# Deformable convolution on one core: the sampling matrices are split pixel by pixel and turned by DMA, and the pipeline works in steps twice as large

## The chip, the cores and the metric

One core of a Trainium2 chip. The metric is the device time of one execution in microseconds (us): 4269.75 us for the kernel before, the median of 3 runs (4259.26 to 4272.78).

## What is computed

The input is a batch of 32 images of 192 channels and 32 x 32 pixels in f32. Cut to what matters:

```python
x = x + attention(groupnorm(x))            # 4 heads' channel attention: q, k, v, softmax over channels, out
v = groupnorm(x)
offset = clip(conv3x3(v, off_w) + off_b, -8, 8)          # 2 x 9 values per pixel
mask = 2 * sigmoid(conv3x3(v, mask_w) + mask_b)          # 9 values per pixel
y = deformable_conv3x3(v, offset, mask, proj_w) + proj_b # bilinear samples at the shifted taps, times weights
x = x + gelu(batchnorm(y))                 # batchnorm: mean and variance over all 32 images
```

## The kernel before

The images go one after another through a loop of two images per turn (`images`, L336 to L349). The deformable convolution is written as matrix products. For an image's chunk of 128 pixels (4 rows, 8 chunks) and each row of taps ky, **Z** = the pixels times the projection weights of three taps (576 columns) is made by TensorE (`z_product`, L628 to L640), in two halves of 288 columns. **S** is the sampling matrix: for each output pixel and tap, the bilinear weight on each of 256 pixels around it (8 rows). It is an outer product of a row part `ay` and a column part `bx`, and GpSimd makes it with the output pixel on the partitions (`sT`, L1323). TensorE needs the source pixel on the partitions, so it turns S with f32 transposes against an identity matrix (`turn_s`, L642 to L651, three of 128 x 128 per unit) into a PSUM bank. Both S and Z are then kept as two f16 halves: ScalarE casts to the high half (`split_s` L883, `split_z` L848), VectorE subtracts it from the f32 value for the low half (`split_s` L1139, `split_z` L1134). `s_product` (L662 to L670) adds nine products of 192 columns into one accumulator bank.

The unit of work is one (tile of output pixels, ky, chunk c): 48 units for an image. In unit u TensorE turns S of unit u + 2, waits for both halves of S of unit u, multiplies, and makes Z of group u + 10 (`part1`, L728 to L754). The other engines keep the same order in queues of their own. Two PSUM banks hold Z and two hold turned S, so TensorE can be two groups ahead of the halves' makers. Every six units a tile of 128 output pixels is done: ScalarE copies the accumulator out (L906 to L910) and the next tile's first product waits for that (`y_pm`, L658).

**Preparation of the next image** (`part0`, one function on each engine) is cut into the same 48 units and interleaved: in unit u of image b every engine does part u of image b + 1. The parts with work: 0 to 5 statistics; 6 to 10 normalisation and its halves (ScalarE four passes of 1024 columns); 12 to 22 attention up to the combined matrix, a chain that goes to and fro between TensorE, ScalarE and VectorE; 23 to 29 the result x1 and its statistics; 30 to 36 the second normalisation, its halves and shifted copies (VectorE, `move`); 38 and 39 the offset convolution (216 products on TensorE); 40 to 46 the row and column parts of S ("hats": `ay`, `bx`). Three more column hats of the current image are made at units 4, 16 and 28 (`column_hats`). SyncE loads x of the next image and stores x1 and y. After all images the batchnorm constants are made, and a last stage streams y and x1 through the core.

Each image ends with a branch on a flag: only if an offset is larger than the 256 pixels allow is `far_pass` run. With these inputs no instruction of it is in the trace.

Of the kernel before, what the change touches and what calls it, by code (L numbers as in the profile page):

```python
# [35 lines left out]
P = 128  # L36
C, H, W = 192, 32, 32
N = H * W
CB = C - P
# [12 lines left out]
UNITS = 6 * TILES  # L52
HEAD_SCALE = float((C // 4) ** (-0.5))
# [29 lines left out]
def build(nc, x, w_qkT, w_v, w_outT, b_out, w_off, b_off, w_proj, proj_b, gamma, beta,  # L83
# [6 lines left out]
    with ExitStack() as ctx:  # L90
# [94 lines left out]
        zps = bank("zps", (P, 2, 512))  # L185
        sps = [bank(f"sps{i}") for i in range(2)]
# [56 lines left out]
        s_ps = sem("s_ps")  # L243
        s_hi = sem("s_hi")
        s_lo = sem("s_lo")
        sz_done = sem("sz_done")
# [89 lines left out]
        def images(program, eng):  # L336

            part0, part1, weights_ready = program  # L340
            for u in range(SLOTS):
                part0(u, 0, 0)
                if u == 15:
                    weights_ready()
            part1(0, 0, True)
            with eng.Fori(1, NB - 2, 2) as b:
                part1(b, 1, True)
                part1(b + 1, 0, True)
            part1(NB - 1, (NB - 1) % 2, False)  # L349
# [7 lines left out]
        AHEAD = 10  # L357
        FAR_Z = 2 * AHEAD
        FAR_SLOT = S_RING - 1
# [8 lines left out]
        def z_piece(z, g, par):  # L368

            half = g % 2 * (KO // 2)  # L370
            return z[:, tile_at(g // 6, par), g % 6 // 2, half:half + KO // 2]
# [37 lines left out]
        def _(sp):  # L409
# [12 lines left out]
            def attended(b, more=True):  # L422
                sp.wait_ge(x1_sb, 4 * b + 4)
                sp.dma_start(x1_dram[b, 0:P], x1[:, 0]).then_inc(x1_stored, 16)
                sp.dma_start(x1_dram[b, P:C], x1[0:CB, 1]).then_inc(x1_stored, 16)
                if more:
                    load_x(b + 1)

            def convolved(b):
                sp.wait_ge(y_final, b + 1)  # L430
                sp.dma_start(y_dram[b, 0:P], ych[:, 0]).then_inc(y_stored, 16)
                sp.dma_start(y_dram[b, P:C], ych[0:CB, 1]).then_inc(y_stored, 16)

            attended(0)
            with sp.Fori(1, NB - 2, 2) as b:
                attended(b)
                convolved(b - 1)
                attended(b + 1)
                convolved(b)
            attended(NB - 1, False)  # L440
            convolved(NB - 2)
# [21 lines left out]
            convolved(NB - 1)  # L463
# [19 lines left out]
        def _(pe):  # L483
# [136 lines left out]
            def z_group(g, b, par):  # L620
# [3 lines left out]
                if g >= 2 or not first(b):  # L624
                    pe.wait_ge(z_lo, UNITS * b + g - 1)
                z_product(g, par, par).then_inc(z_ps, 1)

            def z_product(g, par, of):  # L628

                j, ky = tile_at(g // 6, par), g % 6 // 2  # L630
# [3 lines left out]
                o = zps[:, g % 2, 0:KO // 2]  # L634
                n = slice(g % 2 * KO // 2, (g % 2 + 1) * KO // 2)
                pe.matmul(o, at(0), wpr_h[:, 0, ky, n], start=True, stop=False)  # L636
                pe.matmul(o, at(0), wpr_l[:, 0, ky, n], start=False, stop=False)  # L637
                pe.matmul(o, at(1), wpr_h[:, 0, ky, n], start=False, stop=False)  # L638
                pe.matmul(o, at(2), wpr_h[:, 1, ky, n], start=False, stop=False)  # L639
                return pe.matmul(o, at(2), wpr_l[:, 1, ky, n], start=False, stop=True)  # L640

            def turn_s(u, b):  # L642
                t, ky, c = u // 6, u % 6 // 2, u % 2
                if c == 0:
                    pe.wait_ge(st_made, 24 * b + 3 * t + ky + 1)
                if u >= 2 or not first(b):
                    pe.wait_ge(s_lo, UNITS * b + u - 1)
                g = (3 * t + ky) % ST_RING
# [4 lines left out]
            def convolve(u, b, par):  # L653
                i, ky, c = u // 6, u % 6 // 2, u % 2
                pe.wait_ge(s_lo, UNITS * b + u + 1)
                if i + c < CHUNKS and (c == 1 or i == 0):
                    pe.wait_ge(z_lo, UNITS * b + 6 * (i + c) + 2 * ky + 2)
                if u % 6 == 0 and (i > 0 or not first(b)):  # L658
                    pe.wait_ge(y_pm, TILES * b + i)
                s_product(u % S_RING, tile_at(i + c, par), ky, u % 6 == 0, u % 6 == 5).then_inc(sz_done, 1)  # L660

            def s_product(slot, j, ky, start, stop):  # L662

                for kx in range(3):
                    z = slice(kx * C, (kx + 1) * C)
                    s_h, s_l = sh[:, slot, kx], sl[:, slot, kx]
# [17 lines left out]
            def far_pass(b, par, more):  # L684
                pe.wait_ge(s_lo, UNITS * (b + 1) + 2 * more)
# [10 lines left out]
                if more:  # L696
                    pe.wait_ge(z_lo, UNITS * (b + 1) + AHEAD)
                    first_chunks(par, 0)
                    pe.wait_ge(fz_lo, FAR_Z * b + AHEAD)
                for t in range(TILES):  # L700
                    for ky in range(3):
                        pe.wait_ge(f_st, 24 * b + 3 * t + ky + 1)
                        for v in far_of(t, ky):
# [3 lines left out]
                            for kx in range(3):  # L707
                                mm = pe.transpose(sps[v % 2][:, kx * P:(kx + 1) * P],
# [681 lines left out]
```

## Time and profile before

| | us |
|---|---|
| median of the runs | 4269.75 |
| span of the profiled execution | 4284.4 |
| TensorE busy, share | 3630.2, 85% |
| VectorE | 2649.3, 62% |
| ScalarE | 2110.5, 49% |
| GpSimd | 1410.9, 33% |
| mean granted TensorE clock | 0.939 of full speed |

The profiled execution's own time is its span, 4284.4 us; it lies 14.65 us above the median of the runs. PE is TensorE, ACT ScalarE, DVE VectorE, POOL GpSimd, SP SyncE; L650 is line 650 of the kernel before.
### The profile page before, as it was taken

The page shows a single profiled execution, that of the slowest core. Times are in us where ns is not written, and L with a number is a line of the kernel's source. Part 1 is how long each engine was busy: PE and PEld are TensorE (multiplying, and loading weights), DVE is VectorE, ACT ScalarE, POOL GpSimd, SP SyncE. Part 2 cuts the span into 40 slices and gives each one's busy share as a digit, 9 for nine tenths or more (in the row PEclk, how much of TensorE's full clock was granted, in tenths as well). Part 3 has the DMA queues.
Part 4 walks back from the last instruction along what each step waited for, and adds up shares of the span by engine and source line. Part 5 has one row for each costly group of instructions (what it writes and reads, how often), then busy time and mean ns, then how long its engine had stood idle before and what let it go on. Part 6 is the DMA issues. An engine that isn't in the chain of part 4 may idle for free.

```text
span 4284.4 us, 109949 instructions
## 1 busy us (share of the span) xinstructions
PE 3630.2 (85%) x38338; PEld 3094.4 (72%) x38338; DVE 2649.3 (62%) x5834; ACT 2110.5 (49%) x4790; POOL 1410.9 (33%) x1165
## 2 busy tenths in 40 slices
PE   3999898999989899998989989898998989899700
PEld 2787777877777778777777877777787777778700
DVE  3666666666666666666666666666666666666522
ACT  1555554555455455545545554554555455445432
POOL 1333332333333233333333333333333333333311
PEclk8999999999999999999999999999999999999955
DMA  2000000000000000000000000000000000000298
GB/s 59 18 27 10 28 27 20 27 27 27 10 27 27 20 27 26 27 10 27 27 20 27 26 27 16 21 27 20 27 26 27 21 16 27 27 20 16 60 361 301
DMA packets 50975, 172.85 MB, mean 40 GB/s; under 512 B 9664, under 2 KB 10880, under 8 KB 50176
## 3 DMA queue, kind: packets, MB, share of 16 engines
q1 hardware_dynamic: 39584, 136.75, 10.6%
q0 software_dynamic: 7168, 25.17, 1.5%
q8 instruction: 426, 6.98, 0.7%
q14 instruction: 373, 3.06, 0.2%
q10 hardware_dynamic: 3424, 0.90, 0.1%
HBM read 87.29 MB, written 75.50 MB: 38 GB/s over the span
## 4 chain that ended last, share of the span: by engine, by line
PE 63%; DVE 13%; issue 13%; ACT 4%; DMA 4%; DVEq 1%; ACTq 1%; SPq 1%; POOL 0%; POOLq 0%
PE sps L650 10%; PE acc L667 6%; PE acc L668 6%; PE acc L669 6%; PE l L578 4%; PE zps L636 3%; DVE zl L1136 3%; PE zps L640 3%; PE zps L637 3%; PE zps L638 3%; PE zps L639 3%; DMA xn<-x_scratch 2%; DVE sl L1142 2%; DVE ych L1204 2%; PE l L510 1%
## 5 line engine op out<-in xcount | busy, mean ns | idle before, releaser
L1323 POOL TENSOR_TENSOR sT<-ay,bx 128x768 f32<-128x768 f32 x768 | 1148.1, 1505 | 1615.3 <-PE sps L650 1547.9
L1142 DVE TENSOR_TENSOR sl<-sps,sh 128x384 f16<-128x384 f32 x1536 | 847.1, 552 | 743.7 <-ACT sh L887 740.3
L887 ACT CAST sh<-sps 128x384 f16<-128x384 f32 x1536 | 741.7, 483 | 915.4 <-PE sps L650 905.9
L667 PE MATMUL acc<-zh,sh 128*128 128x192 f16 x4608 | 1155.7, 251 | 0.3 <-ACT ypm L910 0.3
L668 PE MATMUL acc<-zl,sh 128*128 128x192 f16 x4608 | 1155.5, 251 | 0.0
L669 PE MATMUL acc<-zh,sl 128*128 128x192 f16 x4608 | 1155.2, 251 | 0.0
L650 PE MATMUL sps<-eye,sT 128*128 128x128 f32 x4608 | 808.0, 285 | 322.0 <-issue 218.2
L853 ACT CAST zh<-zps 128x288 f16<-128x288 f32 x1536 | 620.1, 404 | 699.6 <-PE zps L640 672.6
L1136 DVE TENSOR_TENSOR zl<-zps,zh 128x288 f16<-128x288 f32 x1536 | 693.9, 452 | 423.0 <-ACT zh L853 415.7
L650 PEld LDWEIGHTS sps<-eye,sT 128*128 128x128 f32 x4608 | 544.5, 143 | 451.9 <-issue 229.4
L667 PEld LDWEIGHTS acc<-zh,sh 128*128 128x128 f16 x4608 | 459.0, 100 | 37.5 <-issue 35.9
L668 PEld LDWEIGHTS acc<-zl,sh 128*128 128x128 f16 x4608 | 459.1, 100 | 20.9
L669 PEld LDWEIGHTS acc<-zh,sl 128*128 128x128 f16 x4608 | 459.1, 100 | 1.6
L636 PE MATMUL zps<-wpr_h,x_hi_a 128*128 128x288 f16 x1344 | 392.1, 292 | 0.8 <-DVE zl L1136 0.3
L637 PE MATMUL zps<-wpr_l,x_hi_a 128*128 128x288 f16 x1344 | 390.8, 291 | 0.0
L638 PE MATMUL zps<-wpr_h,x_lo_a 128*128 128x288 f16 x1344 | 390.1, 290 | 0.0
L639 PE MATMUL zps<-wpr_h,x_hilo_b 128*128 128x288 f16 x1344 | 389.7, 290 | 0.0
L640 PE MATMUL zps<-wpr_l,x_hilo_b 128*128 128x288 f16 x1344 | 389.7, 290 | 0.0
L1307 POOL TENSOR_TENSOR bx<-off,cx_sb 128x576 f32<-128x576 f32 x128 | 155.3, 1213 | 459.4 <-DVE off L1103 459.4
L1289 POOL TENSOR_TENSOR rstd<-gvar,mhalf 128x2 f32<-128x2 f32 x64 | 44.8, 700 | 582.0 <-DVE gvar L993 582.0
L578 PE MATMUL l<-wof,x2s_hi_a 128*128 128x54 f16 x1536 | 183.0, 186 | 9.8 <-DVE x2w_hilo_b L1009 9.8
L578 PE MATMUL l<-wof,x2s_lo_a 128*128 128x54 f16 x1536 | 182.8, 186 | 0.0
(200 smaller groups left out, 6498.0 us busy)
## 6 DMA issues: line engine op xcount, KB each, us to landing
xin<-in_x SPq DMA_DIRECT2D x32, 512.0 KB, 5.5
xin<-in_x SPq DMA_DIRECT2D x64, 256.0 KB, 5.9
x_scratch<-x SPq DMA_DIRECT2D x32, 512.0 KB, 2.8
y_scratch<-ych SPq DMA_DIRECT2D x32, 512.0 KB, 2.7
zh<-y_scratch SPq DMA_DIRECT2D x20, 512.0 KB, 11.0
zl<-x_scratch SPq DMA_DIRECT2D x20, 512.0 KB, 12.0
out<-zh POOLq DMA_DIRECT2D x20, 512.0 KB, 8.8
x_scratch<-x SPq DMA_DIRECT2D x32, 256.0 KB, 3.5
```

The source lines that it names most:

```text
L578: mm = pe.matmul(o, src[:, row * W:(row + ROWS_T) * W], wof[:, m, k].rearrange("p i j -> p (i j)"), start=(k == 0 and n == 0), stop=(k == ...
L636: pe.matmul(o, at(0), wpr_h[:, 0, ky, n], start=True, stop=False)
L637: pe.matmul(o, at(0), wpr_l[:, 0, ky, n], start=False, stop=False)
L650: mm = pe.transpose(sps[u % 2][:, kx * P:(kx + 1) * P], sT[:, g, kx, c * P:(c + 1) * P], eye32[:, :])
L667: pe.matmul(acc[:, 0:C], s_h, zh[:, j, ky, z], start=start and kx == 0, stop=False)
L668: pe.matmul(acc[:, 0:C], s_h, zl[:, j, ky, z], start=False, stop=False)
L669: mm = pe.matmul(acc[:, 0:C], s_l, zh[:, j, ky, z], start=False, stop=stop and kx == 2)
L853: act.copy(z_piece(zh, g, par), zps[:, g % 2, 0:KO // 2]).then_inc(z_hi, 1)
L887: act.copy(sh[:, u % S_RING].rearrange("p k n -> p (k n)"), sps[u % 2][:, 0:3 * P]).then_inc(s_hi, 1)
L1136: dve.tensor_tensor(z_piece(zl, g, par), zps[:, g % 2, 0:KO // 2], z_piece(zh, g, par), ALU.subtract)\
L1142: dve.tensor_tensor(one(sl), sps[u % 2][:, 0:3 * P], one(sh), ALU.subtract).then_inc(s_lo, 1)
L1323: pool.tensor_tensor(sT[:, p % ST_RING].rearrange("p k (r x) -> p k r x", r=R), a, x_, ALU.mult)\
```

## The change

The transposes on TensorE go away. GpSimd now makes S with all 256 source pixels of three taps in one f32 tile (as before), ScalarE and VectorE split it into f16 halves where it lies, 768 columns at once, and SyncE turns both halves, 1536 columns of f16, with one DMA transpose into `sT`. Work goes in 24 steps of what were two units. Z is made as 2 x 288 columns in two neighbouring PSUM banks and its halves are made 576 columns at once. Look-ahead is 5 steps for Z and 3 for S (4 for GpSimd). The ring of f32 S and the ring of its halves have 2 places each, the ring of turned S has 4. Preparation is shifted by 6: step p of image b does parts 2p + 6 and 2p + 7 of image b + 1, and from step 21 on the first six parts of image b + 2; both parts stand together behind the step's products. SyncE issues nothing but transposes during the images; loads of x and stores of x1 and y move to ScalarE's queue (x1 and x at part 34, y at step 5). The column hats of the current image are made at steps 1, 7 and 13. GpSimd's reserved scratch for descriptors is 4096 bytes instead of the default.

```diff
+STEPS = 3 * TILES
+SHIFT = 6
...
-        ST_RING = 3
-        sT = sb("sT", [P, ST_RING, 3, R * W])
-        S_RING = 3
-        sh = sb("sh", [P, S_RING, 3, P], F16)
-        sl = sb("sl", [P, S_RING, 3, P], F16)
+        S_RING = 2
+        s32 = sb("s32", [P, S_RING, 3 * R * W])
+        spm = sb("spm", [P, S_RING, 2, 3 * R * W], F16)
+        T_RING = 4
+        sT = sb("sT", [P, T_RING, 12, P], F16)
...
-        zps = bank("zps", (P, 2, 512))
-        sps = [bank(f"sps{i}") for i in range(2)]
+        zps = bank("zps", (P, 4, 512))
...
+        def prepare(part0, u, b, par, more):
+
+            if u + SHIFT < SLOTS:
+                if more:
+                    part0(u + SHIFT, b + 1, 1 - par)
+            elif more == 2:
+                part0(u + SHIFT - SLOTS, b + 2, par)
...
-        AHEAD = 10
+        AHEAD = 5
+        S_AHEAD = 3
...
+            def turn_s(p, b):
+                sp.wait_ge(s_lo, STEPS * b + p + 1)
+                sp.sem_inc(lo_seen, 1)
+                if p >= T_RING or not first(b):
+                    sp.wait_ge(sz_done, STEPS * b + p - T_RING + 1)
+                    sp.sem_inc(slot_free, 1)
+                sp.dma_start_transpose(sT[:, p % T_RING], spm[:, p % S_RING].rearrange("p i n -> p (i n)"))\
+                  .then_inc(turned(b, p)[0], 16)
...
-            def turn_s(u, b):
...
-                for kx in range(3):
-                    mm = pe.transpose(sps[u % 2][:, kx * P:(kx + 1) * P], sT[:, g, kx, c * P:(c + 1) * P], eye32[:, :])
-                mm.then_inc(s_ps, 1)
...
+            def convolve(p, b, par):
+                i, ky = p // 3, p % 3
+                pe.wait_ge(*turned(b, p))
+                if p % 3 == 0 and (i > 0 or not first(b)):
                     pe.wait_ge(y_pm, TILES * b + i)
...
+                for p in range(STEPS):
+                    convolve(p, b, par)
+                    if p == 4:
+                        offset_max(b)
+                    if p + AHEAD < STEPS:
+                        z_group(p + AHEAD, b, par)
                     elif more:
...
+                        z_group(p + AHEAD - STEPS, b + 1, 1 - par)
+                    if p % 6 == 1 and p > 6:
+                        turn_y(p // 6 - 1, b)
+                    for u in (2 * p, 2 * p + 1):
+                        prepare(part0, u, b, par, more)
...
+                if u == 34:
+                    store_x1(b)
+                    if not isinstance(b, int) or b < NB - 1:
+                        load_x(b + 1)
...
+            def split_s(p, b):
+                act.wait_ge(st_made, STEPS * b + p + 1)
+                if p >= S_RING or not first(b):
+                    act.wait_ge(*turned(b, p - S_RING))
+                act.copy(spm[:, p % S_RING, 0], s32[:, p % S_RING]).then_inc(s_hi, 1)
...
+                        split_s(p + S_AHEAD - STEPS, b + 1)
...
+                    if p % 6 == 1 and p < 18:
+                        column_hats(p // 6 + 1, b, par)
+                    if p % 3 == 2:
+                        t = p // 3
+                        act.wait_ge(sz_done, STEPS * b + p + 1)
...
+            def split_s(p, b):
+                dve.wait_ge(s_hi, STEPS * b + p + 1)
+                dve.tensor_tensor(spm[:, p % S_RING, 1], s32[:, p % S_RING], spm[:, p % S_RING, 0], ALU.subtract)\
+                   .then_inc(s_lo, 1)
...
+                if p >= S_RING or not first(b):
+                    pool.wait_ge(s_lo, STEPS * b + p - S_RING + 1)
...
-    nc = bacc.Bacc("TRN2", target_bir_lowering=False, num_devices=1)
+    nc = bacc.Bacc("TRN2", target_bir_lowering=False, num_devices=1, dynamic_dma_scratch_size=4096)
```

## Rows read from the trace of the kernel before

**Rows 1.** One image: stretch, length, busy PE, PEld, DVE, ACT, POOL, clock, DMA share, GB/s.

```profile
1059.50:1182.70 123.20, 112.99 (x1198) 96.18 (x1198) 80.54 (x181) 64.26 (x150) 42.61 (x34) 0.97 0.08 24
```

**Rows 2.** Timeline of TensorE through one unit (start, duration).

```profile
1062.54 0.49 PE L650 MATMUL sps<-eye,sT 128*128 128x128 f32 x3
...
1062.87 0.25 PE L667 MATMUL acc<-zh,sh 128*128 128x192 f16 x1
...
1063.61 0.29 PE L636 MATMUL zps<-wpr_h,x_hi_a 128*128 128x288 f16 x1
...
1064.22 0.49 PE L650 MATMUL sps<-eye,sT 128*128 128x128 f32 x3
```

**Rows 3.** Waits of TensorE in one image (1236.0 to 1357.5): total, times, longest.

```profile
PE sps L650 <- issue: 8.4, 1, 8.4
...
PE l L509 <- DVE gram L1056: 0.6, 1, 0.6
```

**Rows 4.** Stretches of parts 30 to 37 and 40 to 47 of one image.

```profile
1311.65:1328.51 16.86, 14.29 (x138) 12.27 (x137) 14.45 (x27) 11.58 (x24) 9.53 (x8) 1.00 0.12 24
1338.10:1352.80 14.70, 13.98 (x141) 12.27 (x137) 10.16 (x30) 9.92 (x26) 8.74 (x7) 1.00 0.01 2
```

**Rows 5.** ScalarE's timeline: hats, an eviction, casts and normalisation.

```profile
1246.73 0.69 ACT L844 ACTIVATE bx<-bx 128x576 f32<-128x576 f32 x1
...
1250.15 0.32 ACT L909 COPY ypm<-acc 128x192 f32<-128x192 f32 x1 [0.26 <-PE acc L669]
...
1250.69 0.40 ACT L853 CAST zh<-zps 128x288 f16<-128x288 f32 x1
...
1253.81 0.47 ACT L887 CAST sh<-sps 128x384 f16<-128x384 f32 x1
1254.17 0.41 ACT L853 CAST zh<-zps 128x288 f16<-128x288 f32 x1
1254.46 1.26 ACT L777 ACTIVATE xh_a<-xin,nbias,rstd 128x1024 f16<-128x1024 f32 x1
1255.60 0.48 ACT L887 CAST sh<-sps 128x384 f16<-128x384 f32 x1
```

**Rows 6.** Groups of the whole run: busy, mean ns of one, idle before.

```profile
L1142 DVE TENSOR_TENSOR sl<-sps,sh 128x384 f16<-128x384 f32 x1536 | 847.1, 552 | 743.7 <-ACT sh L887 740.3
L887 ACT CAST sh<-sps 128x384 f16<-128x384 f32 x1536 | 741.7, 483 | 915.4 <-PE sps L650 905.9
...
L853 ACT CAST zh<-zps 128x288 f16<-128x288 f32 x1536 | 620.1, 404 | 699.6 <-PE zps L640 672.6
L1136 DVE TENSOR_TENSOR zl<-zps,zh 128x288 f16<-128x288 f32 x1536 | 693.9, 452 | 423.0 <-ACT zh L853 415.7
```

**Rows 7.** Timeline of the softmax, parts 18 to 21: VectorE and ScalarE.

```profile
1282.00 0.61 DVE L1042 TENSOR_REDUCE nmax<-l 128x1 f32<-128x192 f32 x2 [0.89 <-PE l L510]
...
1284.12 0.43 ACT L812 ACTIVATE gram<-l,nmaxs 128x192 f32<-128x192 f32 x1
...
1286.65 1.05 DVE L1056 TENSOR_SCALAR gram<-gram,rinv 128x192 f32<-128x192 f32 x2
```

**Rows 8.** DMAs: issue of three loads on SyncE; issue to landing, median us.

```profile
1181.45 2.15 SPq L412 DMA_DIRECT2D xin<-in_x  x3
...
xin<-in_x SPq DMA_DIRECT2D x64, 256.0 KB, 5.9
x_scratch<-x SPq DMA_DIRECT2D x32, 512.0 KB, 2.8
```

**Rows 9.** A 2-us window of TensorE, idle since 1227.7: granted clock 0.94.

```profile
1230.00:1232.00 2.00, 0.00 (x0) 0.94 0.07 12
```

**Rows 10.** The same copy on VectorE beside GpSimd and without it.

```profile
1071.87 1.69 POOL L1323 TENSOR_TENSOR sT<-ay,bx 128x768 f32<-128x768 f32 x1 [2.23 <-PE sps L650]
...
1072.16 1.45 DVE L1008 COPY x2w_hi_a<-x_hi_a 128x96 f16<-128x96 f16 x1
...
1080.32 0.17 DVE L1008 COPY x2w_hilo_b<-x_hilo_b 128x96 f16<-128x96 f16 x1
```

More of the change, by code:

```diff
@@ L242, in build @@
         st_made = sem("st_made")
-        s_ps = sem("s_ps")
         s_hi = sem("s_hi")
         s_lo = sem("s_lo")
+        lo_seen = sem("lo_seen")
+        slot_free = sem("slot_free")
+        s_turned = [sem(f"s_turned{i}") for i in range(T_RING)]
         sz_done = sem("sz_done")
@@ L420, in _, with part1 @@
             sp.dma_start(cx_sb[:, :, :], cx.rearrange("p (k x) -> p k x", k=TAPS)).then_inc(const_in, 16)
[L422 to L441, printed above, removed]
+            def turn_s(p, b):
[6 more added lines that the diff above has]
+                  .then_inc(turned(b, p)[0], 16)
+            def part1(b, par, more):
+                if first(b):
+                    for p in range(S_AHEAD):
+                        turn_s(p, b)
+                for p in range(STEPS):
+                    if p + S_AHEAD < STEPS:
+                        turn_s(p + S_AHEAD, b)
+                    elif more:
+                        turn_s(p + S_AHEAD - STEPS, b + 1)
+            images((lambda u, b, par: None, part1, lambda: None), sp)
             def load(dst, src, q, slot, i):
@@ L848, in split_z @@
             def split_z(g, b, par):
[L849 to L853 removed]
+                if g % 3 == 0 and not first(b):
+                    act.wait_ge(sz_done, STEPS * (b - 1) + 3 * (last_use(g // 3) + 1))
+                act.wait_ge(z_ps, STEPS * b + g + 1)
+                act.copy(z_piece(zh, g, par), z_bank(g)).then_inc(z_hi, 1)
             def far_pass(b, par, more):
[L856 removed]
+                act.wait_ge(sz_done, STEPS * (b + 1))
                 act.wait_ge(yt_ps, 4 * (b + 1))
@@ L910, in part1 @@
                         act.copy(ypm[:, t % 4, C:2 * P], acc[:, P:C]).then_inc(y_pm, 1)
-                    if u + AHEAD < UNITS:
-                        split_z(u + AHEAD, b, par)
+                    if p + AHEAD < STEPS:
+                        split_z(p + AHEAD, b, par)
                     elif more:
-                        split_z(u + AHEAD - UNITS, b + 1, 1 - par)
-                    if more:
-                        part0(u, b + 1, 1 - par)
+                        split_z(p + AHEAD - STEPS, b + 1, 1 - par)
+                    for u in (2 * p, 2 * p + 1):
+                        prepare(part0, u, b, par, more)
+                    if p == 5 and not first(b):
+                        store_y(b - 1)
                 where_far(flag, act, b, par, more, far_pass, (fz_hi, FAR_Z), (fs_hi, FAR_UNITS), (fy_pm, TILES))
@@ new lines, in part1 @@
+            def part1(b, par, more):
+                lead = S_AHEAD + 1
+                if first(b):
+                    for p in range(lead):
+                        make_s(p, b, par)
+                for p in range(STEPS):
+                    if p + lead < STEPS:
+                        make_s(p + lead, b, par)
+                    elif more:
+                        make_s(p + lead - STEPS, b + 1, 1 - par)
+                    if p in (0, 4, 10):
+                        column_distance((0, 4, 10).index(p) + 1, b, par)
+                    for u in (2 * p, 2 * p + 1):
+                        prepare(part0, u, b, par, more)
```

227 lines of the change are left out of this document (99 added, 128 removed).

## Prediction

> **What bounds the kernel now.** I read the busy time of an image first. TensorE works 113.0 of 123.2 us, VectorE 80.5, ScalarE 64.3, GpSimd 42.6 [rows 1]. So TensorE sets the pace, and I looked at what it does in a unit and at what it waits for. The timeline of a unit shows 0.33 us of transposes (start to start), 0.74 of products with S, 0.61 of Z: 1.68 in all, 80.6 us for the 48 units of an image [rows 2]. TensorE's waits in an image are one fetch of instructions of 8.4 us at the loop's turn (about half that at the other image end), 0.6 us for the softmax [rows 3], 2.6 us in the second normalisation (16.86 less 14.29) and 0.7 us with the hats [rows 4]. In those last two stretches VectorE and ScalarE are nearly full: 14.5 and 11.6 of 16.9 us. That is the row to remember: TensorE is the bound on average, but not everywhere by much.
>
> **What TensorE saves.** 144 transposes of an image go: 48 x 0.33 = 16 us. A step costs 2 x (0.74 + 0.61) = 2.7 us where two units cost 3.36. If nothing else moved, 31 images would give 500 us.
>
> **What the other engines pay.** In a full queue ScalarE starts a cast of S every 0.36 us, one of Z every 0.29, a normalisation pass every 1.14 [rows 5]. The slope from 288 to 384 columns is 0.82 ns a column on ScalarE and 1.04 on VectorE [rows 6]. So a 768-wide cast costs 0.36 + 384 x 0.82 ns = 0.68, a 576-wide one 0.53; on VectorE (0.47 and 0.36 now, durations less the same 0.09 of overlap) 0.87 and 0.66. That is a little less than today in all: 29 us for 31 on ScalarE, 37 for 40 on VectorE. Totals stay far under 107 us; they decide nothing. The order in the queues does, because a step now carries two preparation parts at once and has 20% less TensorE time over it. I walked the queues of one image with these costs, three times where it matters.
>
> *Step 3.* The first product of a tile waits until ScalarE has copied out the tile before. ScalarE's queue from the image's start: Z's cast can begin at 2.85 us (the first step's end); cast 0.53; parts 6 and 7, two passes 2.3; cast of S 0.7; hats 2 x 0.68 = 1.36 [rows 5]; cast of Z 0.53; parts 8 and 9, 2.3; cast of S 0.7; eviction 0.54 [rows 5]: 11.8 us. TensorE arrives after 3 x 2.68 = 8.0. It waits 3.8 us. Today the hats stand at unit 4, before an eviction that has no passes ahead of it, and nothing is waited for.
>
> *Steps 5 to 8, attention.* Parts of a pair now follow each other with no product between. Part 20 (VectorE) and 21 (TensorE) share step 7: behind part 18's product come the maxima (0.61 and a small scaling, with the product's own tail 1.0), the exponentials (two of 0.43 and their sums, 0.92) [rows 7], ScalarE's cast of S, hats and cast of Z (0.7 + 1.35 + 0.53), VectorE's half of Z 0.66 and the scaling (1.05 and the reciprocals, 1.3) [rows 7]: 6.5 us and some 0.4 of semaphores. TensorE has 1.5 + 1.2 + 0.45 us to do, so it waits 3.7, where it waits 0.6 now. Parts 22 and 23 share step 8: a cast and a subtraction with a small one behind each, 1.7 us, hidden by a whole unit today. Parts 16 and 17: 1.2 us for 0.5.
>
> *Steps 12 to 16.* The four passes meet the hats of step 13 again. From the end of step 12: cast of Z 0.53, two passes 2.3, cast of S 0.7, hats 1.35, cast of Z 0.53, two passes 2.3, cast of S 0.7, eviction 0.54, together 9.0; TensorE is at the next tile after two steps, 5.4, and waits 3.4 to 3.6. In step 14 ScalarE also issues five DMAs, 3.2 us in its queue (three take 2.15 on SyncE [rows 8]), with its casts and thereby VectorE's copies behind them; the offset convolution then waits for the last copy, 2.8 us. Together 6.2 for 2.6 now [rows 4].
>
> *Steps 17 to 21.* Parts 40 and 41, 44 and 45 share steps, so ScalarE stands waiting for VectorE's offsets and distances (some 2 us twice by the walk) with its casts queued behind it, and the hats of part 42 besides; a late half of Z (0.7), a late turn (0.9) and a late eviction (3.3) cost 4.9 us for 0.7 now. *Group statistics* at steps 11 and 23: 3.0 for about 0.8.
>
> Waits in all 3.8 + 3.7 + 1.7 + 1.2 + 6.2 + 4.9 + 3.0 = 24.5 us where today's walk gives 5: 19.5 more, against 16 less: **+3.3 us an image**. The same walk over today's order gives waits of about 1.1, 0.3 and 1.1 us at units 36 to 38, which is how the 2.6 us of [rows 4] come about.
>
> *The clock.* TensorE had been idle for about 4 us (since 1227.7) when the granted clock began to fall from 2.4 GHz, 0.94 in that window [rows 9]. The new waits end just short of that; I add 0.2 us an image.
>
> **Costed at nothing.** The fetches at the image ends stay: branch and loop are the same. SyncE has only 24 transposes an image in 127 us. GpSimd's tile (1.5 us a step) is released by VectorE and stays ahead. The later load of x (part 34 instead of 28) still leaves seven steps. The stores of y at step 5 are 1 us of ScalarE's queue behind an eviction. The smaller scratch and the untouched last stage give nothing. If a cover fails, it is ScalarE's: each us there before an eviction is a us of TensorE.
>
> *The turn itself* has no row. It moves 384 KB: the nearest rows are a store of 512 KB, 2.8 us to landing, and a load of 256 KB behind another, 5.9 [rows 8]. I take 3.5, nearer to the store, since nothing is queued ahead of it. A place in the ring of halves is used every second step: 5.4 us in the shortest steps less 1.6 of casts, more in the long ones, so up to about 5 us it costs nothing; at 5.9 about 1.5 us an image; below 2.8 it gains nothing. The Trainium skill (DMA: Bandwidth & Descriptors, "Latency and other measured facts") states 261 GB/s for one kernel's DMA transposes; as an estimate from that page 384 KB would move in 1.5 us, and the sum would be the same. No run here shows it.
>
> **VectorE and GpSimd.** A copy of 96 columns took 1.45 us instead of 0.17 and ended with GpSimd's multiplication, at 1073.56 [rows 10]: one of the two stood still until the other was done. The new subtraction of S has both inputs in SBUF, while today's has one in PSUM. So it costs 0.87 alone and up to 1.48 more if GpSimd's tile has just begun. I take 0.87, because GpSimd starts its tile when a subtraction ends, three engines' turns before the next. The Trainium skill (SBUF — State Buffer, "SBUF: two separate sides") says that a VectorE operation with two SBUF inputs and a GpSimd operation hold a shared port in turn, for a whole instruction; by that rule every subtraction is exposed, and the trace agrees for the copy.
>
> **The sum.** 31 images x 3.5 = +109. The first starts 4 us later (a transpose must land). The last has no preparation beside it, so it saves most of the 16: -12. +101 on the profiled 4284, which is 15 above the median: 4370.
>
> **Rivals.**
> *TensorE keeps the pace (faster).* The place is the three evictions (3.8 + 3.4 + about 3.3 us). If ScalarE reaches them in time, 10.5 us fall away and an image takes 7 less: 4370 - 31 x 10.5 = 4045. For it: ScalarE is busy only half the time. Against: 11.8 us of queue over 8.0. It decides from 3.3 us an image on. 22%.
> *VectorE meets GpSimd.* If a subtraction waits on average 0.55 us, 13 us of VectorE an image, half of it in stretches that are late, +6: 4560. 10%.
> *The turn is the bound.* Where a transpose holds the queue for more than a step, 24 of them are the image: at 6.5 us, 156 us an image and 5300; it decides from 5.3 us a transpose on. The Trainium skill (VectorE: DVE Perf Modes, "The three transpose paths") gives 1309 ns for 128 x 128 by DMA and 390 on TensorE; twelve in a row would be 15.7 us, an estimate from the page that speaks against the change. Nothing in the rows bears out that they go one by one. 6%.
> *No difference:* the transposes leave TensorE but new waits give back just the 16 us, 4270: the change does not do what it says. 6%.
>
> **How the numbers follow.** Forecast 56%, rivals 22, 10, 6, 6. A measurement of this kernel tells 0.3%, 13 us. Faster 22%, within 6%, slower 72%. Its own range is 4300 to 4460 (a us of error an image and the landing's bounds). To leave out no more than two in ten it reaches down to 4120, which leaves out about half of the faster rival, and up to 4600, over VectorE's.
>
> **What would show it.** Right: an image of 126 to 128 us; TensorE busy near 97 of it; waits of products (first of a tile) for ScalarE's copy of the accumulator, 3 to 4 us, three an image; one of 3 to 4 for the scaled softmax; offset convolution waiting for VectorE's copy; transposes landing in 3 to 5 us. Wrong: images under 120 us with those waits absent, products waiting for the DMA instead, or subtractions of S at 1.3 us and more.

## The result and the profile after

The changed kernel takes **4540.5 us** (median of 4 runs, 4512.4 to 4557.7) beside 4268.8 for the kernel before (4259.3 to 4272.8): ratio 1.064, 95% interval 1.060 to 1.068. Slower, as forecast (4370, range 4120 to 4600), but by 272 us where the sum had 101.

The page of the changed kernel: the span, the busy times, TensorE's granted clock and the DMA engines in slices, and DMA queue 1, which carries the transposes.

```profile
span 4556.1 us, 93343 instructions
PE 3341.9 (73%) x33730; PEld 2754.6 (60%) x33730; DVE 2420.0 (53%) x4298; ACT 1903.8 (42%) x3254; POOL 1421.9 (31%) x1165
PEclk8888889898888989888898988889888988998955
DMA  2545556454655555465555555555545555555699
q1 hardware_dynamic: 1220272, 356.77, 47.1%
```

TensorE is at work for less time than before, the DMA engines are half busy all the way, and the clock row shows more 8s than 9s. How much that is, a stretch of 24 images tells, cut at the same point of the softmax in both kernels. First the kernel before, then the changed one (columns as in [rows 1]):

```profile
410.81:3400.68 2989.87, 2714.73 (x28755) 2315.96 (x28754) 1933.10 (x4320) 1535.38 (x3553) 1022.84 (x816) 0.97 0.08 24
```

```profile
430.99:3635.95 3204.96, 2499.21 (x25299) 2063.86 (x25297) 1758.46 (x3168) 1378.96 (x2401) 1029.88 (x816) 0.89 0.55 92
```

Divided by 24, an image took 124.6 us, TensorE busy 113.1 and idle 11.5; it takes 133.5 now, busy 104.1 and idle 29.4. So 9.0 us more an image; 31 images make 278, nearly all of the 272. The sum had busy 16 us less and idle 19.5 us more.
TensorE's waits over the whole run (total, times, longest) answer to [rows 3]:

```profile
PE acc L687 <- ACT ypm L941: 332.6, 96, 4.3
PE acc L687 <- issue: 190.4, 31, 9.8
PE l L535 <- DVE gram L1089: 90.2, 32, 3.4
PE l L604 <- issue: 74.5, 21, 5.8
PE l L590 <- DVE mt_l L1095: 48.9, 32, 1.5
PE l L604 <- DVE x2w_hilo_b L1042: 27.3, 32, 9.8
```

Three waits an image for the copied accumulator (L941), 10.4 us together (forecast 3.8 + 3.4 + 3.3); the softmax 2.8 (3.7); parts 22 and 23 1.5 (1.7). The stalls at the image ends, which the prediction took for fetches of instructions, are still there (second row). New and not in the sum is the fourth row: in the middle of the offset convolution (L604) TensorE stands still for about 3.5 us in two images of three, and this view names nothing that it waited for.

What a wait does to the clock: windows of 1 us around the wait for the accumulator at step 15, 1415.0 to 1418.1 (second number: busy TensorE; third last: granted clock).

```profile
1414.00:1415.00 1.00, 1.00 (x9) 0.59 (x6) 0.26 (x1) 1.00 (x3) 0.65 (x1) 1.00 0.02 8
1415.00:1416.00 1.00, 0.03 (x1) 0.00 (x0) 1.00 (x2) 1.00 (x2) 0.83 (x1) 1.00 0.79 135
...
1417.00:1418.00 1.00, 0.00 (x0) 0.00 (x0) 1.00 (x5) 1.00 (x4) 0.00 (x0) 0.94 1.10 280
1418.00:1419.00 1.00, 0.92 (x6) 0.88 (x7) 1.00 (x2) 0.57 (x2) 0.23 (x1) 0.50 1.03 401
```

Nearly 3 us after TensorE went idle the clock drops to 1.2 GHz, and the next 3.4 us of products run at it. At the softmax (TensorE idle from 1378.3) it drops after 2.0 us already:

```profile
1378.30:1380.30 2.00, 0.04 (x1) 0.00 (x0) 1.10 (x3) 1.21 (x2) 1.12 (x1) 1.00 0.11 22
1380.30:1381.10 0.80, 0.00 (x0) 0.00 (x0) 0.69 (x5) 0.00 (x0) 0.36 (x1) 0.52 1.13 210
1381.10:1387.10 6.00, 5.97 (x24) 3.82 (x25) 0.96 (x1) 1.26 (x3) 0.00 (x1) 0.50 0.19 34
```

The length of a wait alone does not settle it. The softmax wait is 2.8 us in 31 of the 32 images. The clock falls 2.0 to 2.5 us into it in some, 0.4 to 2.3 us after TensorE is at work again in others, and in three not at all. Over the 24 images 112 waits of 2.6 to 4.5 us began at full clock: 53 had the fall inside, 50 up to 2.5 us behind them, 9 had none. Of 104 waits of 0.35 to 1.3 us none had a fall at either place.

Finally the landings: the extremes over 558 transposes (min, median, max).

```profile
DMA to landing us min/median/max: 3.6/3.7/14.4
```

The median is close to the 3.5 that was taken. But two transposes an image, issued 3.6 and 8.1 us after the first of the five transfers of part 34 (two stores of x1, three loads of x), land after 10 to 14 us; the last of the three loads takes 12.7 in the median.

### The profile page after: what moved, and what is told of

It is laid out like the page before. It is cut to its first block, busy times and chain, and to the rows that moved or that the text cites. A ratio compares the mean times of both kernels' runs of the same rounds, so it can differ in the third digit from the quotient of the medians.

```text
span 4556.1 us, 93343 instructions
## 1 busy us (share of the span) xinstructions
PE 3341.9 (73%) x33730; PEld 2754.6 (60%) x33730; DVE 2420.0 (53%) x4298; ACT 1903.8 (42%) x3254; POOL 1421.9 (31%) x1165
## 4 chain that ended last, share of the span: by engine, by line
PE 41%; issue 17%; DVE 15%; ACT 11%; DMA 7%; DVEq 4%; ACTq 4%; SPq 1%; POOL 0%; POOLq 0%
PE acc L687 5%; PE acc L688 5%; PE acc L689 5%; PE l L604 3%; DMA sT<-spm 3%; ACT zh L870 3%; ACT spm L903 3%; DVE stats L1007 2%; PE zps L663 2%; PE zps L664 2%; DMA xn<-x_scratch 2%; PE zps L665 2%; PE zps L667 2%; PE zps L666 2%; ACTq L862 2%
## 5 line engine op out<-in xcount | busy, mean ns | idle before, releaser
L1354 POOL TENSOR_TENSOR s<-ay,bx 128x768 f32<-128x768 f32 x768 | 1136.2, 1481 | 2392.3 <-DVE spm L1174 2006.4
L687 PE MATMUL acc<-zh,sT 128*128 128x192 f16 x4608 | 1237.3, 269 | 558.7 <-ACT ypm L941 332.6
L1174 DVE TENSOR_TENSOR spm<-s,spm 128x768 f16<-128x768 f32 x768 | 757.3, 986 | 1107.9 <-ACT spm L903 903.0
L688 PE MATMUL acc<-zl,sT 128*128 128x192 f16 x4608 | 1239.5, 269 | 20.5 <-issue 20.5
L689 PE MATMUL acc<-zh,sT 128*128 128x192 f16 x4608 | 1239.4, 269 | 0.0
L870 ACT CAST zh<-zps 128x576 f16<-128x576 f32 x768 | 489.6, 638 | 1039.1 <-PE zps L667 1038.5
L1169 DVE TENSOR_TENSOR zl<-zps,zh 128x576 f16<-128x576 f32 x768 | 579.5, 754 | 592.7 <-ACT zh L870 588.9
L687 PEld LDWEIGHTS acc<-zh,sT 128*128 128x128 f16 x4608 | 491.1, 107 | 661.4 <-ACT ypm L941 322.0
L903 ACT CAST spm<-s 128x768 f16<-128x768 f32 x768 | 638.5, 832 | 589.7 <-DMA sT<-spm 396.4
L688 PEld LDWEIGHTS acc<-zl,sT 128*128 128x128 f16 x4608 | 492.8, 107 | 49.8 <-issue 23.1
L689 PEld LDWEIGHTS acc<-zh,sT 128*128 128x128 f16 x4608 | 496.7, 108 | 8.4
L604 PE MATMUL l<-wof,x2s_hi_a 128*128 128x54 f16 x1536 | 187.6, 189 | 27.3 <-DVE x2w_hilo_b L1042 27.3
L604 PE MATMUL l<-wof,x2s_hilo_b 128*128 128x54 f16 x1536 | 187.1, 188 | 3.1 <-issue 3.1
L604 PE MATMUL l<-wof,x2s_lo_a 128*128 128x54 f16 x1536 | 187.2, 189 | 2.1 <-issue 2.1
L604 PE MATMUL l<-wof,x_hi_a 128*128 128x54 f16 x768 | 145.0, 189 | 50.4 <-issue 50.4
L604 PEld LDWEIGHTS l<-wof,x2s_hi_a 128*128 128x128 f16 x1536 | 137.0, 98 | 56.3 <-DVE x2w_hilo_b L1042 36.8
```

Source lines behind the costliest of these rows:

```text
L604: mm = pe.matmul(o, src[:, row * W:(row + ROWS_T) * W], wof[:, m, k].rearrange("p i j -> p (i j)"), start=(k == 0 and n == 0), stop=(k == ...
L687: pe.matmul(acc[:, 0:C], s_h, zh[:, j, ky, z], start=start and kx == 0, stop=False)
L688: pe.matmul(acc[:, 0:C], s_h, zl[:, j, ky, z], start=False, stop=False)
L689: mm = pe.matmul(acc[:, 0:C], s_l, zh[:, j, ky, z], start=False, stop=stop and kx == 2)
L870: act.copy(z_piece(zh, g, par), z_bank(g)).then_inc(z_hi, 1)
L903: act.copy(spm[:, p % S_RING, 0], s32[:, p % S_RING]).then_inc(s_hi, 1)
```

## The experiments

Each kernel was timed in three rounds beside the kernel before; its time is read against that kernel's 4273 to 4277 us in the same rounds, and against the change's ratio of 1.064. The change's own runs lie 45 us apart, so differences between two variants are good to some 20 us.

### Is it the clock?

Useless products ahead of four waits, into a bank that is free there:

```diff
+FILLS = 4
...
+def keep_busy(bank, n):
+    for _ in range(n):
+        pe.matmul(bank[:, 0:2 * C], eye32[:, :], wqk[:, 0], start=True, stop=True)
...
 # convolve
+if p in (3, 15, 21):
+    ...
+    keep_busy(l0[1 if p == 3 else 0], FILLS)
...
 # part 21
+keep_busy(l0[1], FILLS - 1)
 pe.wait_ge(prob_sb, b + 1)
```

> The changed kernel, and TensorE does useless f32 products (four of 384 columns, 2.6 us; three ahead of the softmax) just before the four places where it waits 2.8 to 4.1 us for another engine; nothing else differs. Clock theory: the missing time is the granted clock, which falls to 0.5 5.5 times an image (once in the kernel before) and stretches TensorE's busy time from the 97 us that the sum had to 104. The dips behind these four waits go, those behind the two fetch stalls stay: 3 dips an image or fewer, mean clock 0.92 or more, useful TensorE work about 4 to 5 us an image shorter, 4400 to 4460 us. If part of what is gained turns into longer waits at ScalarE's queue, 4480. Rival (the waits and the transposes' traffic themselves are the price, the clock is only their sign): 4540, or slower by what the products overrun, up to 4580.

Measured: **4416.0 us** (4397.6 to 4450.2), 1.031 (1.027 to 1.036): more work on the engine that bounds the kernel, and 125 us less. 24 images of it:

```profile
416.66:3536.07 3119.41, 2600.47 (x26019) 2098.05 (x26017) 1772.86 (x3168) 1376.73 (x2400) 1031.64 (x816) 0.93 0.57 95
```

Busy 108.4 us an image, of which the 15 products are 9.7 (0.65 each from one start to the next), leaves 98.6 for the useful work against 104.1: 5.5 us. The clock falls 2.1 times an image for 5.5, and is at half for some 17 us for 29. The useful products are the same, and their time fell together with the half-clock time; the theory stands. Of the 5.5 us, 1.9 came back as longer waits, most of them in the offset convolution: 2.3 us an image for VectorE's copies (0.9 before), and 110.7 us in all in the unnamed stall (74.5 before). So filling does not touch that stall.

### Is it the order of the queues?

The shift of preparation is one constant (`SHIFT = 7`, `SHIFT = 3`).

> The changed kernel with image preparation shifted by 7 units instead of 6, so that parts are paired 21+22, 41+42, 43+44 and not 20+21, 22+23, 40+41, 44+45. Queue theory (where ScalarE's passes and hats fall against the evictions sets the waits): the walk of the queues gives 4.4 us an image less wait, with fewer dips of the clock on top 6 to 8: 4300 to 4400 us. Rival (the waits come from the transposes themselves, their landing or their traffic, or from the wider steps whatever the pairing): within 1% of the changed kernel, 4500 to 4580.

> The changed kernel with image preparation shifted by 3 units instead of 6. Queue theory: the walk gives 5.4 us an image less wait than with 6; with fewer dips of the clock 4280 to 4400 us, about as the shift by 7. Rival (a larger shift is what hides the softmax and the moved copies): slower than the changed kernel, 4560 to 4650, since the copies of x2 reach the first step of the next image 1.5 steps later. Rival (transposes and not the order): 4500 to 4580.

Measured: **4459.7** (1.042, 1.038 to 1.047) for 7, above the 4300 to 4400 expected; **4404.0** (1.029, 1.025 to 1.033) for 3, at the edge. Both are better than 6. The walk's 4.4 and 5.4 us an image less wait came out as 3.2 and 5.4 us of image time, but that is not the walk's doing alone: in neither trace does TensorE stall in the offset convolution without a named cause, which is 2.4 us an image of the 4.3 and 4.1 us of idle time that went. (The expectation for the run with 36 dummy transposes, below, says that both showed that stall; their waits do not have it.) So the order of the queues gave clearly less than the walk had, and why the stall is absent no run shows. The clock stayed at 0.89 and 0.90, with 5.5 and 4.6 falls an image. Fewer waits are no gain in clock as long as those left are long: with 7, the wait for the accumulator at step 15 alone grew from 3.0 to 6.3 us.

The shift alone, in the kernel before:

> The kernel before with one part of the change alone: image preparation runs 6 units earlier, S is still turned by TensorE, units stay single. The walk of the queues gives an image 1 us longer than before: 4270 to 4330 us. If instead the shift by itself is what brings ScalarE's passes onto the evictions, 3 to 5 us an image: 4370 to 4430. If the shift is a gain that the rest of the change gives back: 4200 to 4250.

Measured: **4290.2** (1.0044, 1.0030 to 1.0058; 10 runs). Clear of noise, but 0.4% only, as the walk had it: moving the preparation costs next to nothing as long as it stays in single units.

The wider eviction undone, in the changed kernel:

```diff
-act.copy(z_piece(zh, g, par), z_bank(g)).then_inc(z_hi, 1)
+act.copy(z_piece(zh, g, par)[:, 0], z_bank(g)[:, 0])
+act.copy(z_piece(zh, g, par)[:, 1], z_bank(g)[:, 1]).then_inc(z_hi, 1)
```

and the same on VectorE.

> The changed kernel with one part undone: ScalarE and VectorE evict Z in two pieces of 288 columns instead of one of 576, at the same places of their queues. ScalarE's queue gets about 0.14 us longer a step and VectorE's 0.13. Queue theory: the walk gives 2.6 us an image more, 4600 to 4650 us. Rival (ScalarE and VectorE have slack, 42% and 53% busy; what waits there is order alone): 4530 to 4560.

Measured: **4554.8** (1.066, 1.063 to 1.069), the rival's number; the interval overlaps that of the change. The walk was wrong here: it turned 0.14 us a step on ScalarE into 2.6 us an image, and the waits for the accumulator and the softmax grew by 0.4 us together (339.6 and 94.5 us in all for 332.6 and 90.2). The 576-wide eviction is neither the loss nor a gain.

### Is it the transposes?

From the second image on, a transfer of 4 bytes a partition instead of each transpose; S is not turned, so the products take stale halves:

```diff
-sp.dma_start_transpose(sT[:, p % T_RING], ...)
+sp.dma_start(sT[:, p % T_RING, 0, 0:2], spm[:, p % S_RING, 0, 0:2])
```

> The changed kernel, but from the second image on SyncE issues a transfer of 4 bytes a partition in place of each DMA transpose: S is not turned (the products take what lies in the ring), all waits and their order stay, the packets go from some 1600 a transfer to 128. Traffic theory (1.2 million small packets slow the instruction fetches and the loads, or the landing of 3.7 us is on the path): fetch stalls shorter, 4.0 and 8.5 us at the image ends and 4 us in the offset convolution down by half, and 4350 to 4450 us. Queue and clock theory (the waits are ScalarE's queue; the landing has slack): 4500 to 4540, at most 1% below the changed kernel, with the three waits for the copied accumulator as long as before.

Measured: **4386.9** (1.026, 1.022 to 1.030), 154 us less than the change: the time that the traffic theory gave, and more than the queue theory allowed. The three waits for the accumulator are all there, and the stall in the offset convolution is gone but for one: what is left is the wait for VectorE's copies. Waits of TensorE in that kernel:

```profile
PE acc L690 <- ACT ypm L944: 330.7, 94, 4.3
PE acc L690 <- issue: 181.0, 31, 9.1
...
PE l L607 <- DVE x2w_hilo_b L1045: 25.7, 32, 9.8
```

The stalls at the image ends stay (181.0 for 190.4), against the traffic theory. So the transposes cost something beside the waits, and the stall that went stands just behind the transfers of x. To see whether that is their traffic as such, the kernel before got transposes that nobody reads:

```diff
+sp.wait_ge(spare_in, 16 * (36 * b + v))
+sp.dma_start_transpose(spare[:, :], dummy_src).then_inc(spare_in, 16)
```

> The kernel before, and SyncE beside it turns a constant f16 tile by DMA transposes, 36 of 128 x 1024 an image (the bytes of the change's 24 of 128 x 1536), into a tile that nobody reads; no other engine waits for them. Traffic theory (the sum costed the fetches of instructions at nothing; the shift by 7 and by 3 units showed the stall in the offset convolution again and the run without transposes did not): TensorE gets a new fetch stall of 2 to 5 us in most images, or the stalls at the image ends grow, 4320 to 4420 us. Rival (the packets matter only to loads that somebody waits for, which here are early): within 0.5% of the kernel before, 4250 to 4290.

Measured: **4536.5** (1.063), as slow as the change itself. It looks like proof of the traffic theory and is none. SyncE's own waits, and one of VectorE's:

```profile
SPq L445 <- DMA spare<-wpr_h: 2125.4, 1084, 6.4
DVE ych L1222 <- DMA y_scratch<-ych: 91.3, 22, 8.6
```

36 transposes one after the other, each waiting for the one before, are the whole image: in the page they are 81% of the chain that ended last. The stores of y behind them in SyncE's queue were late, and VectorE waited for them, which it never does in the kernel before. (The next expectation blames the loads of x; those landed at least 23 us before they were needed.) The run priced a full queue. With 24 an image the queue has room:

> The kernel before with 24 turned constant tiles of 128 x 1024 an image beside it (two thirds of the change's bytes). In the run with 36, SyncE waited 2125 us for its own earlier transposes, was the chain for 81% of the span and held the loads of x back, so that its 4536 us price a full queue and not the traffic. With 24, each 3.1 us to landing, SyncE has 75 to 80 us of work in 125. Theory (traffic by itself costs the engines little; what costs is a transfer that somebody waits for landing late): 4270 to 4310 us. Rival (packets slow the fetches of instructions wherever they are): new stalls of TensorE without a named releaser, 4330 to 4420.

Measured: **4309.4** (1.008, 1.006 to 1.011). With the DMA engines 0.41 busy (0.08 without) an image is 0.6 us longer, and what grew are the stalls at the image ends (252.8 us in all for 218.2, the longest 11.3 for 8.8). That is a cost of the traffic, but a small one; the time lies at the upper edge of the forecast. These are two thirds of the change's bytes; the change's full traffic without a full queue was not tried.

The collision is tested on the changed kernel by moving the five transfers apart, one a step (`move_x` issues the two stores and three loads in turn):

```diff
-if u == 34:
-    store_x1(b); load_x(b + 1)
+if u == 34:
+    act.wait_ge(x1_sb, 4 * b + 4)
+if u in (34, 36, 38, 40, 42):
+    move_x(u // 2 - 17, b)
```

> The changed kernel, but the two stores of x1 and the three loads of x stand at parts 34, 36, 38, 40 and 42, one a step, and not all at part 34. Collision theory: in the traces two transposes an image, issued within some 5 us of these five transfers, land after 9 to 13 us (all others after 3.7), and TensorE stalls 4 us in the offset convolution there; spread out, transposes land under 7 us, the stall goes, one dip of the clock less: 3 to 5 us an image, 4400 to 4450 us. Rival (the stall is any traffic against the fetch, whatever its density): within 0.7% of the changed kernel, 4510 to 4570.

Measured: **4427.2** (1.038, 1.034 to 1.041), 113 us less, with the same bytes. 24 images of it, and its landings:

```profile
420.97:3506.66 3085.69, 2449.52 (x25299) 2026.33 (x25297) 1753.70 (x3168) 1378.64 (x2400) 1031.49 (x816) 0.91 0.53 96
```

```profile
DMA to landing us min/median/max: 3.6/3.7/8.6
```

The slowest transpose lands after 8.6 us, the small loads after 3.5 (9.9 before spreading); of the stalls at L604 without a named cause one of 1.1 us is left. An image is 5.0 us shorter: 2.9 of it idle time, 2.1 busy, with 4.7 falls of the clock for 5.5.

What TensorE stood still for, the waits do not name, but the DMA records of the changed kernel do. One of its stalls:

```profile
1430.63 0.18 PE L604 MATMUL l<-wof,x2s_hilo_b 128*128 128x54 f16 x1
1435.80 0.23 PE L604 MATMUL l<-wof,x_hi_a 128*128 128x54 f16 x1 [4.99 <-issue]
```

Queue 8, of kind `instruction` in the page, brings blocks of 16 KB. One of them has its packets from 1433.36 to 1434.26, and TensorE goes on 1.5 us later. In all 21 stalls the last packet of such a block ends 1.3 to 1.6 us before TensorE goes on, and 14 of the 21 stand before the same product, the 193rd of the convolution's 216; in the kernel with filling, which has more instructions in an image, 26 of 28 stand before the 135th or 136th. So the stall is a block of instructions that came late, and the burst is what made it late: spread, the blocks of queue 8 come as before, and in time.

### Do the two add up?

> The changed kernel in its own order (shift by 6) with both remedies: the useless f32 products ahead of four waits (alone 125 us less) and the transfers of x spread over five steps (alone 113 us less). If clock and collision are what the sum left out, the rest is the sum's own: its queue waits, 4370, less the 4 us an image by which they were overrated, 4250 to 4330 us, and the two gains add. Rival (the two are one: the stall that goes is itself a dip of the clock): 4360 to 4420.

Measured: **4291.2** (1.0029, 1.0012 to 1.0047; 10 runs).

```profile
406.74:3396.86 2990.12, 2562.74 (x26019) 2061.22 (x26017) 1753.68 (x3168) 1379.98 (x2400) 1032.85 (x816) 0.95 0.53 99
```

Busy 106.8 less 9.7 of filling is 97.1 us of useful work, which is 113.1 less 16: with the clock kept up, the transposes' whole 16 us appear. 125 and 113 add to 238, and 249 went, the same within the noise. With both remedies the clock falls 1.3 times an image. What is left of the change is what its queues make it wait, part of it now spent in useless products, and that is no more than the transposes had cost: within 0.3% of the kernel before.

### Can it be made faster than before?

Three edits of order on the changed kernel, found with the same walk: shift by 3; ScalarE copies the accumulator ahead of its cast of S; the whole offset convolution in part 39.

```diff
-SHIFT = 6
+SHIFT = 3
 # ScalarE, step p: these two change places
+if p % 3 == 2: ... act.copy(ypm ..., acc ...)
 split_s(p + S_AHEAD, b)
 # TensorE
-if 38 <= u < 40:
+if u == 39:
```

> The changed kernel with three edits of order: preparation shifted by 3 units instead of 6, ScalarE copies the accumulator ahead of its cast of S in the same step, and the whole offset convolution stands at part 39. Queue theory: by the walk an image has 4 us less wait than with the shift by 3 alone (127.9 us measured): 124 us, 4270 to 4310 us for all, the waits for the moved copies of x2 (4.5 us) gone. Rival (clock and traffic give it back: every wait over 2 us still ends in a half-clock stretch): 126.5 to 128 us an image, 4360 to 4400.

Measured: **4534.1** (1.062): far above both. The trace has what neither expected, a transpose that TensorE waits 10 us for in the stretch with the x transfers:

```profile
PE acc L687 <- DMA sT<-spm: 246.1, 48, 11.8
```

```profile
DMA to landing us min/median/max: 3.6/3.7/16.0
```

(both between 500 and 3600 us). The same kernel with the transfers spread:

> The kernel with the three edits of order (shift by 3, accumulator copied first, offset convolution at part 39; 4534 us) and the same spreading of the x transfers. There one transpose an image landed after 12 us and TensorE waited 10 us for it. Collision theory: that wait goes and the walk's 124 us an image come true: 4250 to 4310 us. Rival (the late landing has another cause, such as SyncE's own fetches): 4480 to 4550, the 10 us waits still there.

Measured: **4250.5** (0.994, 0.992 to 0.996; 7 runs), 284 us less from moving five transfers; those waits are down to 45.7 us, the slowest landing to 8.0, an image to 123.6. The collision is the cause, and its price depends on whether TensorE needs just that transpose: in the changed kernel it waited for a late one hardly ever (20.0 us in all), here 10 us in every image.

The order with the filling (three products each ahead of the offsets' maximum, the second group statistics, and the accumulator at steps 15 and 21), without and with the spreading:

> The kernel of the run before this one, with three useless f32 products of 384 columns (1.9 us) ahead of four waits: the maximum of the offsets, the second group statistics, and the copied accumulator at steps 15 and 21. Clock theory: 2 to 4 us an image less, dips behind the two fetch stalls and little else, mean clock over 0.92: 4170 to 4230 us, faster than the kernel before. Rival (the waits grow by what TensorE saves): 4260 to 4300.

> The kernel with the edits of order and the useless products ahead of four waits (4172 us), with the x transfers spread as well. Its landings near the transfers are 6 to 8 us already, so the collision costs it little: 1 to 2 us an image, 4110 to 4160 us. Rival: spreading only lengthens the time in which loads and transposes meet, 4170 to 4220.

Measured: **4172.3** (0.976, 0.973 to 0.979) and **4108.5** (0.963, 0.959 to 0.966). The last is 3.7% faster than the kernel before. The first gained 362 us on the order alone, more than the clock gives: the slowest transpose took 7.7 us instead of up to 16. The traces show why. With the order alone a transpose is issued 1.9 us after the first store of x1, between the stores and the loads, in every image, and lands after 12 to 16 us. With the filling it is issued at the same moment as that store, ahead of the loads, and lands after 6.4 to 7.7. So the products shifted it off the burst, by luck and not by design; in the changed kernel the filling left the transposes at 3.6 and 8.1 us after the store, and they took up to 15.4. Between the two kernels with spread transfers, where no transpose is that late, the filling is worth 142 us, and spreading on top of the filling 64. The last, 24 images:

```profile
399.08:3243.13 2844.05, 2520.81 (x25875) 2041.58 (x25873) 1759.17 (x3169) 1396.01 (x2401) 1057.72 (x816) 0.95 0.58 104
```

Busy 105.0 less 7.7 of filling is 97.3, idle 13.5.

## Why the prediction was right in direction and short in size

Of its own signs of being right, the waits for the accumulator came as described; the image (133.5 us for 126 to 128) and TensorE's busy time (104 for 97) did not.

*TensorE saves 16 us an image.* Right as work: 97.1 and 97.3 us where the clock was kept. In the changed kernel 9 of the 16 were left.

*The walk of the queues, +19.5 us.* Right in kind, a fifth too large: +17.9 measured, but 2.4 of them are the new stall, which the walk did not have, so 15.5 are the walk's. The waits for the accumulator came to 10.4 for 10.5; the softmax was overrated by 0.9, the group statistics (about 2.3 for 3.0) and the copies of x2 (0.6 for 2.8) too. (The text's 3.3 us an image is 24.5 less its items of today, 5.2, less 16; 19.5 less 16 is 3.5, the number that the sum uses.) Waits of 15.5 against 16 saved would have made no difference. So the direction, too, was in part luck: slower came from the two terms that follow, which the sum had at 0.2 and at nothing. The run with both remedies, at 1.003, agrees.

*The clock, +0.2 us: the step that failed.* The prediction read [rows 9], a clock that began to fall 4 us after TensorE went idle, as a bound that waits of 3 to 4 us stay under ("the new waits end just short of that"). One fall, seen after 4 us, says nothing of shorter waits. The same trace had an earlier one: at the end of its first image TensorE is idle from 106.1, and the clock is at full in the first of these windows and at 0.69 on the mean in the next, so it fell 2.7 us into the wait (third last number).

```profile
106.00:108.00 2.00, 0.09 (x1) 1.00 0.00 0
108.00:110.00 2.00, 0.00 (x0) 0.69 0.01 4
```

And at every other image end, after a stall of 4.2 us, the clock fell when TensorE was back at work, 11 times of 12. So the clock's cost should have had a range up to a fall behind each of the new waits. Only waits of 1.1 us were seen to leave the clock up (the row below, of the kernel before).

```profile
1445.60:1446.70 1.10, 0.06 (x1) 0.06 (x1) 1.10 (x4) 0.40 (x1) 0.39 (x1) 1.00 0.00 0
```

Measured in the changed kernel: 5.5 falls an image for 1, some 29 us at half clock for some 8, and 6.8 us more busy time than in the sum; the kernel with filling and the one with both remedies show that it is the clock, a part of it (2.1) behind the stall that the spreading removed. In 31 images 6.8 us are 211 us, more than the whole gap of 170 between 4370 and 4540. The stall adds 2.4 an image, and the waits overrated take 3.7 back: 5.5 in all.

*Fetches costed at nothing: the second step that failed.* Those at the image ends did stay, but the five transfers of x were moved onto ScalarE's queue at one part, and were costed there as time of ScalarE's queue alone (3.2 us), not as a burst that meets the transposes and holds up a block of instructions in the middle of an image. By the run with the transfers spread it costs 5.0 us an image, the clock's part included.

*The turn itself.* 3.5 us taken, 3.7 measured. Right in the median, but the bound of 5.9 was too low for the worst case: 14.4. The estimate of 1.5 us from the 261 GB/s of the Trainium skill (DMA: Bandwidth & Descriptors, "Latency and other measured facts") is less than half of that: a transfer of 4 bytes a partition in its place still took 1.6 to 1.7 us to land. And twelve times the 1309 ns of the Trainium skill (VectorE: DVE Perf Modes, "The three transpose paths") would be 15.7: twelve blocks landed together in 3.7, so here the measurement decides against both readings.

*VectorE and GpSimd.* The subtraction of S was to cost 0.87 us from start to start, 0.96 as a duration. 725 of 768 take 0.94 to 0.99; 39 take 1.4 to 2.2 us, all of them with a GpSimd instruction beside them. By the Trainium skill (SBUF — State Buffer, "SBUF: two separate sides") a VectorE operation with two SBUF inputs and GpSimd's tile can't run side by side; those 39 agree, and they show it better than the prediction's copy, which has one input. That the two seldom meet fits the reason given, since GpSimd starts when a subtraction ends. The mean is 986 ns, and 1019 without the transposes, so they don't slow it.

*Rivals.* The turn as the bound and TensorE keeping pace both fell with the waits of 3 to 4 us, seen where they were forecast. VectorE's, priced at 4560, is near the measured 4540 by coincidence only: its subtractions did not grow. No difference is what the queues alone would have given. No rival said that the waits cost more than their length; it is the mechanism that was missing from the list.

## What to carry to other kernels

Where TensorE is the bound, a wait of 2 to 4 us can cost more than itself: here 4.5 more falls of the clock an image took 7 us of busy time, 1.6 each. So count the waits, not only their sum, and try cheap useless products ahead of those that can't be removed. Don't issue large loads and stores in a burst while short transfers with a deadline are in flight, blocks of instructions among them: one a step cost nothing and gave 113, 284 and 64 us. When a dummy load is added to price a resource, look first at whether its own queue has become the chain. And when a variant is faster, look for what else changed in its trace before crediting the edit.

## What the runs showed of the hardware that was not expected

- The granted clock fell from 2.4 to 1.2 GHz after TensorE had been idle for as little as 2.0 us, and sooner where another wait of 0.7 us or more had gone shortly before; the products behind ran at 1.2 GHz for 3 to 7 us. It also fell up to 2.5 us after TensorE was at work again: behind 50 of 112 waits of 2.6 to 4.5 us, and behind 16 of 55 of 1.3 to 2 us. 15 products of 0.65 us an image ahead of four waits took the falls from 5.5 to 2.1 an image and made the kernel 125 us faster.
- A DMA transpose of 128 x 1536 f16 within SBUF lands in 3.6 to 3.7 us, one of 128 x 1024 in 3.0. Issued 2 to 8 us after the start of a burst of 1.8 MB of stores and loads it takes 7 to 16 us; issued at its start, ahead of the loads, 6.4 to 7.7.
- The DMA engines 0.41 busy with 0.8 million packets under 512 bytes made the kernel before 0.8% slower.
- A burst of transfers can stop TensorE without a data dependence: behind it TensorE stalled 1.7 to 5.8 us inside one run of products, until 1.3 to 1.6 us after a 16 KB block of the queue of kind `instruction` had come. It went without the transposes and with the burst spread (in the other order some 20 stalls of 1 us were left), and it was absent, for a reason that no run shows, with the preparation shifted by 7 or 3.
